# Two more scan states built by TensorE from diagonals that transfers spread, and all turns of h made by transfers

## The chip, the cores and the metric

The kernel runs on one core of one Trainium2 chip. The metric is the device time of one execution in microseconds (us), median of several runs; lower is better. TensorE (PE), VectorE (DVE), ScalarE (ACT), GpSimd (POOL) and the queue of transfers on SyncE (SP) work side by side and meet only at semaphores.

## The reference, cut to what matters

```python
# x (4, 512, 512), ctx (4, 512, 256); d_inner 512, 16 states, dt_rank 16; F = 2048
u   = silu(conv1d(ctx @ in_proj^T) + conv_b)                 # (b, 512 channels, 512 steps)
dt_low, Bm, Cm = split(x_proj @ u)                           # 16 + 16 + 16 rows by 512 steps
dt  = softplus(dt_proj @ dt_low + dt_bias);  A = -exp(A_log)
for l in steps:                                              # for each of 512 channels, 16 states
    state = state * exp(dt[l] * A) + dt[l] * u[l] * Bm[l]
    y[l]  = sum_over_states(state * Cm[l])
x1  = x + tanh(g_xattn) * swap((y + D * u) * silu(layernorm(x)))
out = x1 + tanh(g_ffn) * ffn(layernorm(x1))
# ffn: rmsnorm, 8-bit rounding of rows, ternary weights;
#      h = silu(gate) * up (2048 wide), rounded by its row's maximum, then down (2048 -> 512)
```

## The kernel before

**Units.** The scan is cut into 16 units `s` (`UNITS`), one for each batch `b = s // 4` and group of 128 channels. A unit has 16 states `n`, each a tile of 128 channels by 512 steps. For each state ACT takes the exponential exp(dt A) (L1169, into a PSUM bank), something makes dt u B, DVE runs the recurrence (`tensor_tensor_scan`, L1510), the result is multiplied by C, and PE sums it over the states into `pY` by transposing it there (L515). In text below "scan 7" is the scan of state 7.

**Who makes dt u B.** POOL does it for two states at a time (`times_b`, L889), from a copy of B spread over the partitions (`b_bc`). From unit 5 on (`PE_FROM`) states 4 and 5 (`PE_PAIR = 2`) are made by PE (`db_state`, L562): `duT`, the turned product of dt and u, times a diagonal matrix with B on it (`diag_b`), whose four blocks for each state ACT writes once a batch (`diagonal`, L1200). For these states the exponential goes to SBUF (L1163) and the product to the PSUM bank.

**Who multiplies by C.** DVE for the states 2, 3, 6, 7, 10, 14, 15 (`own`; L1518, with C spread by PE, `c_bcast`, L509), POOL for the pairs 0, 2, 4, 6 (L881) and for state 11 alone (L895).

**The feed-forward part** runs one tile of 128 rows behind: in unit `s` tile `t1 = s - 4` gets its gate and up products (L584), its silu (L1117) and the product with up (`times_up`, L1461); tile `t2 = s - 5` gets its row maximum (`h_max`, L1465), is scaled and rounded on ACT (`scale_h`, L1150), turned by PE in four groups of four blocks (`hq_transpose`, L615), and copied as bf16 to `hqT` by ACT (`copy_hqT`, L1155); tile `s - 6` gets its down product (L633) in the pieces called `fill`, and its output (L1486). For the last tiles (`DMA_FROM = 11` on) the turning is done by a transfer (`turn_h`, L410).

**Order.** All orders are written out by hand: each engine has one list, of which the loops below print the core. In units 5, 6, 7, 9, 10, 11, 13, 14, 15 the tile x is turned early (L578); units 4, 8, 12 start a batch of the feed-forward part (`t1 % NT == 0`), and their lists differ. ACT's exponential for state n waits for the scan three before it (its bank). SP's queue issues the row loads of the next unit, the four broadcasts of B and of C at the end of a batch (`load_b`, `load_c`), and the stores.

Of the kernel before, what the change touches and what calls it, by code (L numbers as in the profile page):

```python
# [5 lines left out]
F32 = mybir.dt.float32  # L6
# [6 lines left out]
P = 128  # L13
# [42 lines left out]
PE_PAIR = 2  # L56
ALONE = 11


def alone(s, n):  # L60
    return s >= PE_FROM and n == ALONE

# [21 lines left out]
def pool_pairs(s):  # L84
    return [c for c in range(NCH) if s < PE_FROM or c != PE_PAIR]

# [9 lines left out]
def by_pe(s, n):  # L96
    return s >= PE_FROM and n // CH == PE_PAIR

# [9 lines left out]
def osc(t):  # L108
# [6 lines left out]
    k_abs k_abv k_ws k_wm k_p1 k_p3 k_clip  # L115
    d_xz0 d_xz1 d_xr0 d_xr1 d_bbc0 d_bbc1 d_bbc2 d_bbc3 d_c0 d_c1 d_c2 d_c3 d_u0 d_u1 d_out0 d_out1
    s_exp s_dbu s_scan s_mul s_pmul s_pytr s_cb s_ytr s_du s_skip s_skd s_dup s_duT s_diag s_dbp s_amul s_aytr d_ca s_sz s_szp s_szT s_y s_x1
    f_bn f_sum f_dev f_ve f_rr f_xn f_xs f_e f_xm f_xqp f_xqT f_gate f_silu f_up f_h f_sq f_mh f_rh f_hs f_hm
    f_hqp f_hqT f_hb f_hp f_hqD f_dn f_o e_y e_x1 e_sq e_max e_ss""".split()
# [13 lines left out]
def build(nc, x, ctxT, g_x, g_f, w_in, w_conv, b_conv, w_xp, w_dt, b_dt, a_log, d_skip, w_gate, w_up, w_down,  # L133
          bc_rows, u_rows, out):
    with ExitStack() as stack:
# [19 lines left out]
        diag_d = sb("diag_d", [P, P])  # L155
# [42 lines left out]
        h_alone = carve(area_f, 4096, L)  # L198
        c_alone = carve(area_f, 7680, L)
# [8 lines left out]
        diag_b = [b_bc[:, CH * PE_PAIR + i, :].rearrange("p (k l) -> p k l", k=NT) for i in range(CH)]  # L208
# [14 lines left out]

        hb = [u_all[:, 2 + 2 * i:4 + 2 * i, :].rearrange("p n l -> p (n l)").bitcast(BF16) for i in range(2)]
# [63 lines left out]
        def _(sp):  # L288
# [14 lines left out]
            def load_c(b):  # L303
                for j, pair in enumerate(pooled(NT * b)):
                    if b and j < len(pooled(NT * b - 1)):
                        sp.wait_ge(S["s_pmul"], POOLED_AT[NT * b - 1] + j + 1)
# [3 lines left out]
            def load_c_alone(b):  # L310
                if b == 1:
# [16 lines left out]
            def load_b(b, quarters=range(4)):  # L328
                for q in quarters:
                    if b:  # L330
                        sp.wait_ge(S["s_dbu"], db_count(b * NT - 1, 2 * q + 1))
                    first = 4 * q + (CH if b * NT >= PE_FROM and 2 * q == PE_PAIR else 0)
                    sp.dma_start(b_bc[:, first:4 * q + 4, :], bc_rows[b, first:4 * q + 4, :].partition_broadcast(P)).then_inc(S[f"d_bbc{q}"], 16)
# [1320 lines left out]
```

## Time and profile before

| | |
|---|---|
| median of 3 runs | 612.5 us (611.86 to 614.23) |
| the profiled execution | 611.89 us, span of its instructions 609.9 us |
| busy share of the span | PE 85%, PE weight loads 59%, DVE 91%, ACT 83%, POOL 85% |
| DMA | 66.32 MB, mean 109 GB/s |
| granted TensorE clock, mean | 0.966 |

Busy time counts instructions, not waits. One unit of the steady part takes 30.3 us, one that starts a batch 33.2 us. "Idle before" in a row is the time that an engine waited just before it, and the name behind it the instruction that ended the wait. Rows of a timeline start with the start time and the busy time; where an engine's instructions overlap, the next can start a little before the one before has ended.

### The profile page before, as it was taken

What the parts mean: (1) busy time and instruction counts of PE and PEld (TensorE: products, weight loads), DVE (VectorE), ACT (ScalarE), POOL (GpSimd) and SP (SyncE); (2) the same over time, 40 slices, a digit from 0 to 9 for tenths busy, and PEclk for the clock granted to TensorE, in tenths of its full rate; (3) what the DMA queues carried; (4) which work ended last, traced back from release to release, by engine and by line L of the source; (5) the groups of instructions that cost most, each with busy time, mean ns of one, the idle gap of its engine ahead of it and who ended that gap; (6) DMA issues with size and microseconds to landing.
All of it is one profiled execution on the core that took longest, in us unless ns stands there. A gap on an engine that the chain in (4) does not pass through costs nothing. (4 is left out here: it accounts for less than half of the span.)

```text
span 609.9 us, 9603 instructions
## 1 busy us (share of the span) xinstructions
PE 516.7 (85%) x3190; PEld 359.8 (59%) x3190; DVE 556.6 (91%) x766; ACT 507.7 (83%) x776; POOL 521.0 (85%) x298
## 2 busy tenths in 40 slices
PE   6999676768675888989879898989789999998997
PEld 2443265747564676767656767675667575764443
DVE  1899989999999899999899999998999999988774
ACT  3879788986999789899978898998798989777773
POOL 1558799999999899999999899999998999973340
PEclk9999859778799999999999999999999999999999
DMA  8992951530661010115521111145411110000323
GB/s 273 403 412 108 325 197 34 192 136 1 240 243 53 0 53 2 35 34 208 203 93 35 34 37 36 35 157 223 121 35 35 36 36 18 1 18 21 84 53 86
DMA packets 38866, 66.32 MB, mean 109 GB/s; under 512 B 12177, under 2 KB 20369, under 8 KB 36002
## 3 DMA queue, kind: packets, MB, share of 16 engines
q1 hardware_dynamic: 38818, 65.72, 30.9%
q8 instruction: 25, 0.41, 0.3%
q14 instruction: 23, 0.19, 0.1%
HBM read 55.49 MB, written 8.13 MB: 104 GB/s over the span
## 5 line engine op out<-in xcount | busy, mean ns | idle before, releaser
L889 POOL TENSOR_TENSOR area_s<-area_s,b_bc 128x1024 f32<-128x1024 f32 x117 | 275.2, 2364 | 14.1 <-DVE u_all L1510 9.9
L515 PE MATMUL pY<-ident,area_s 128*128 128x128 f32 x532 | 87.9, 291 | 54.5 <-DVE area_s L1518 54.5
L584 PE MATMUL pG<-wq_gu,area_f 128*128 128x512 fp8e4 x448 | 108.0, 380 | 4.2 <-ACT area_f L1106 2.9
L1510 DVE TENSOR_TENSOR_SCAN area_s<-pA,area_s 128x512 f32<-128x512 f32 x88 | 105.1, 1205 | 5.1 <-ACT pA L1169 5.1
L515 PEld LDWEIGHTS pY<-ident,area_s 128*128 128x128 f32 x532 | 62.2, 146 | 75.4 <-DVE area_s L1518 67.9
L1169 ACT ACTIVATE pA<-dt_all,a_neg 128x512 f32<-128x512 f32 x145 | 97.7, 682 | 10.7 <-DVE area_s L1510 5.9
L881 POOL TENSOR_TENSOR u_all<-u_all 128x1024 f32<-128x1024 f32 x44 | 103.9, 2361 | 0.2 <-DMA u_all<-bc_rows 0.2
L1518 DVE TENSOR_TENSOR area_s<-area_s,pC 128x512 f32<-128x512 f32 x132 | 87.0, 661 | 0.9 <-DVE area_s L1510 0.8
L509 PE MATMUL pC<-ident,xdT 128*128 128x128 f32 x528 | 84.2, 288 | 3.2 <-DVE area_s L1518 2.0
L584 PEld LDWEIGHTS pG<-wq_gu,area_f 128*128 128x128 bf16 x448 | 41.6, 98 | 48.9 <-ACT area_f L1106 5.2
L509 PEld LDWEIGHTS pC<-ident,xdT 128*128 128x128 f32 x528 | 65.4, 146 | 8.1 <-DVE area_s L1518 6.6
L633 PE MATMUL pT<-wq_dn,area_f 128*128 128x512 fp8e4 x224 | 53.9, 379 | 0.0
L515 PE MATMUL pY<-ident,u_all 128*128 128x128 f32 x352 | 49.6, 287 | 1.7 <-POOL u_all L881 1.7
L515 PEld LDWEIGHTS pY<-ident,u_all 128*128 128x128 f32 x352 | 42.9, 149 | 5.0 <-POOL u_all L881 2.1
L1461 DVE TENSOR_TENSOR area_f<-area_f,pG 128x512 f32<-128x512 f32 x52 | 34.6, 677 | 8.4 <-PE pG L584 6.0
L1169 ACT ACTIVATE pC<-dt_all,a_neg 128x512 f32<-128x512 f32 x57 | 38.9, 683 | 3.3 <-DVE u_all L1510 2.4
L1510 DVE TENSOR_TENSOR_SCAN u_all<-pA,area_s 128x512 f32<-128x512 f32 x33 | 39.5, 1210 | 0.1
L1117 ACT ACTIVATE area_f<-pG,sm 128x512 f32<-128x512 f32 x52 | 34.3, 684 | 4.2 <-PE pG L584 3.3
L834 POOL TENSOR_TENSOR area_s<-area_s 128x511 f32<-128x511 f32 x16 | 20.0, 1273 | 20.8 <-DVE area_s L1348 20.8
L615 PE MATMUL pG<-ident,area_f 128*128 128x128 f32 x176 | 24.0, 278 | 15.9 <-ACT area_f L1155 13.1
L1510 DVE TENSOR_TENSOR_SCAN area_s<-pC,area_s 128x512 f32<-128x512 f32 x29 | 35.0, 1205 | 1.4 <-ACT pC L1169 1.4
L633 PEld LDWEIGHTS pT<-wq_dn,area_f 128*128 128x128 bf16 x224 | 21.9, 98 | 19.7
(218 smaller groups left out, 1123.0 us busy)
## 6 DMA issues: line engine op xcount, KB each, us to landing
b_bc<-bc_rows SPq DMA_DIRECT2D x14, 1024.0 KB, 6.7
area_s<-x SPq DMA_DIRECT2D x32, 256.0 KB, 2.9
u_all<-bc_rows SPq DMA_DIRECT2D x14, 512.0 KB, 6.5
b_bc<-w_gate SPq DMA_DIRECT2D x1, 4096.0 KB, 14.0
dt_all<-x SPq DMA_DIRECT2D x1, 4096.0 KB, 24.3
area_f<-w_up SPq DMA_DIRECT2D x1, 4096.0 KB, 33.6
area_f<-w_down SPq DMA_DIRECT2D x1, 4096.0 KB, 14.9
out<-area_f SPq DMA_DIRECT2D x16, 256.0 KB, 2.1
```

What stands on the lines that cost most here:

```text
L509: mm = pe.transpose(c_bank(s, m)[:, k * P:(k + 1) * P], xdT[:, s // NT, k, NS + n:NS + n + 1].to_broadcast([P, P]), ident[:, :])
L515: mm = pe.matmul(pY[:, k * P:(k + 1) * P], src[:, k * P:(k + 1) * P], ident[:, :], is_transpose=True, start=(first and k == 0), stop=(last ...
L584: mm = pe.matmul(bank, xqT[t % 2][:, k, :], wq_gu[:, k, m, c * GW:(c + 1) * GW], start=(k == 0), stop=(k == NT - 1))
L615: mm = pe.transpose(banks[r % 2][:, k * P:(k + 1) * P], h_of(t)[:, (4 * r + k) * P:(4 * r + k + 1) * P], ident[:, :])
L633: mm = pe.matmul(pT[:, :], hqT[t % 2][:, k, :], wq_dn[:, k, :], start=(k == 0), stop=(k == FK - 1))
L881: gp.tensor_tensor(hp[j], hp[j], c_bc[j], ALU.mult).then_inc(S["s_pmul"], 1)
L889: gp.tensor_tensor(db[c % NDB], du[s % 2].rearrange("p (a l) -> p a l", a=1).to_broadcast([P, CH, L]), b_bc[:, CH * c:CH * c + CH, :], ALU ...
L1117: act.activation(h_of(t)[:, c * GW:(c + 1) * GW], bank, ACT.Silu, scale=col(CS[t % 2])).then_inc(S["f_silu"], 1)
L1169: act.activation(exp_bank(s, n), dt_all[:, s, :], ACT.Exp, scale=a_neg[:, s % NT, n:n + 1]).then_inc(S["s_exp"], 1)
L1461: dve.tensor_tensor(chunk, chunk, bank, ALU.mult).then_inc(S["f_h"], 1)
L1510: dve.tensor_tensor_scan(h, at, dbu, 0.0, ALU.mult, ALU.add).then_inc(S["s_scan"], 1)
L1518: dve.tensor_tensor(p_st[i % NH], h_st[i % NH], c_bank(s, m), ALU.mult).then_inc(S["s_mul"], 1)
```

## The change

States 6 and 7 join 4 and 5: from unit 5 on PE makes dt u B of four states, and POOL of six pairs. The diagonal matrices are no longer written by ACT: in DRAM a tensor `b_spread` is filled with zeros once, then four transfers a batch write the 512 numbers of each state's B onto the diagonals, one number at a time (`spread_b`), and one transfer of 1 MB loads the sixteen blocks (`load_diagonals`). Every h tile up to 10 is turned by two transfers (`turn_whole`), from bf16 halves that ACT writes in place over the f32 ones (`whole_h`); the four groups of PE transposes and the four ACT copies are gone. The diagonal of D is written once for each of the four channel groups and no longer for each unit (`skip`). The products with C are shared out as before. Some PE steps change place: state 7's sum goes behind the gate products, and the broadcasts at a batch's end are issued in another order, behind the two turns.

```diff
-PE_PAIR = 2
-ALONE = 11
+PE_PAIRS = (2, 3)
+BY_PE = tuple(CH * c + i for c in PE_PAIRS for i in range(CH))
+NB = len(BY_PE)
+ALONE = (11,)
...
-        diag_d = sb("diag_d", [P, P])
+        diag_d = sb("diag_d", [P, NT, P])
+        zeros = sb("zeros", [P, L])
...
-        diag_b = [b_bc[:, CH * PE_PAIR + i, :].rearrange("p (k l) -> p k l", k=NT) for i in range(CH)]
+        diag_b = [b_bc[:, n, :].rearrange("p (k l) -> p k l", k=NT) for n in BY_PE]
...
+        h_int = [carve(area_f, 1024 * i, F // 4, BF16) for i in range(2)]
...
+            def zero_spread():
+                sp.wait_ge(S["k_zero"], 1)
+                sp.dma_start(b_spread.rearrange("b j (p f) -> p (b j) f", p=P),
+                             zeros[:, :].rearrange("p (a f) -> p a f", a=1).to_broadcast([P, (BATCH - 1) * NB, L])).then_inc(S["c_zero"], 16)
+
+            def spread_b(b):
+
+                sp.wait_ge(S["c_zero"], 16)
+                for j, n in enumerate(BY_PE):
+                    spots = b_spread[b - 1, j].rearrange("(k r) -> k r", k=NT)[:, 0:P * P:P + 1]
+                    sp.dma_start(spots, bc_rows[b, n].rearrange("(k p) -> k p", k=NT), allow_slow_non_contiguous=True).then_inc(S[f"c_bd{b}"], 16)
+
+            def load_diagonals(b):
+                sp.wait_ge(S[f"c_bd{b}"], 16 * NB)
                 if b == 1:
-
-                    sp.wait_ge(S["k_p3"], 2 * NW + 1)
+                    sp.wait_ge(S["s_dbu"], db_count(PE_FROM - 1, PE_PAIRS[-1]))
                 else:
-                    sp.wait_ge(S["s_amul"], b * NT - PE_FROM)
-                sp.dma_start(c_alone, bc_rows[b, NS + ALONE].partition_broadcast(P)).then_inc(S["d_ca"], 16)
+                    sp.wait_ge(S["s_dbp"], NB * (b * NT - PE_FROM))
+                sp.dma_start(b_bc[:, BY_PE[0]:BY_PE[0] + NB, :].rearrange("p j (k l) -> p (j k) l", k=NT),
+                             b_spread[b - 1].rearrange("j (k p l) -> p (j k) l", k=NT, p=P)).then_inc(S["d_bd"], 16)
...
+            zero_spread()
             load_x(3)
             load_u(3)
+            spread_b(1)
+            def turn_whole(t):
+
+                past(sp, S["f_dn"], t - 1)
+                for i in range(2):
+                    past(sp, S["f_hqD"], 32 * t + 16 * i)
+                    sp.wait_ge(S["f_ha"], 2 * t + i + 1)
+                    sp.dma_start_transpose(hqT[t % 2][:, i * FK // 2:(i + 1) * FK // 2, :], h_int[i]).then_inc(S["f_hqD"], 16)
+
             for s in range(NT, UNITS):
                 load_z(s)
                 load_x(s)
                 load_u(s)
+                b = s // NT
                 if s % NT == 0:
-                    load_b(s // NT)
-                    load_c(s // NT)
-                    load_c_alone(s // NT)
+                    load_b(b, (0, 1))
+                if s >= 6:
+                    turn_whole(s - 6)
+                if s % NT == 0:
+                    if b > 1:
+                        load_diagonals(b)
+                    load_b(b, (2,))
+                    load_c(b, (0,))
+                    load_b(b, (3,))
+                    load_c(b, (1, 2, 3))
+                    load_c_alone(b)
+                if s == NT:
+                    load_diagonals(1)
+                if s in (NT + 1, NT + 2):
+                    spread_b(s - NT + 1)
                 if s >= 7:
                     store(s - 7)
...
-                pe.wait_ge(S["s_diag"], CH * NT * (s // NT - 1) + NT * (i + 1))
+                pe.wait_ge(S["d_bd"], 16 * (s // NT))
...
                 if t1 % NT:
                     pe.wait_ge(S["f_h"], FC * t1)
                     xq_transpose(t1, pG[0])
+                if s >= PE_FROM:
+                    db_state(s, 2)
                 fill(s, early, 4)
                 y_sum(s, 3)
                 c_bcast(s, 6)
+                if s >= PE_FROM:
+                    db_state(s, 3)
                 y_sum_pooled(s, 0)
-                if t2 >= 0:
-                    if t1 % NT:
-                        pe.wait_ge(S["f_xqT"], t1 + 1)
-                    hq_transpose(t2, 0, pG)
-                    hq_transpose(t2, 1, pG)
                 fill(s, 4, DPARTS)
-                if t2 >= 0:
-                    hq_transpose(t2, 2, pG)
-                    hq_transpose(t2, 3, pG)
                 y_sum(s, 6)
...
                 if t1 % NT:
                     y_sum_pooled(s, 1)
                     c_bcast(s, 10)
-                    y_sum(s, 7)
                     gate(t1, 2)
                     gate(t1, 3)
                 else:
 
                     c_bcast(s, 10)
-                    y_sum(s, 7)
-                    if ALONE in own(s):
-                        c_bcast(s, ALONE)
+                    if s < PE_FROM:
+                        y_sum(s, 7)
+                        c_bcast(s, 11)
                     gate(t1, 2)
                     gate(t1, 3)
                     y_sum_pooled(s, 1)
+                if s >= PE_FROM:
+                    y_sum(s, 7)
                 y_sum(s, 10)
...
-                if s + 1 < UNITS:
+                if 3 in pool_pairs(s + 1) and s + 1 < UNITS:
                     times_b(s + 1, 3)
...
-                if t <= UNITS - NT:
-                    past(act, S["f_hqp"], HR * (t - (1 if t < UNITS - NT else 2)) + HR)
-                else:
+                if t < UNITS - NT and t and c % 2 == 0:
+                    act.wait_ge(S["f_hqD"], 32 * (t - 1) + (32 if c else 16))
+                elif t > UNITS - NT:
                     act.wait_ge(S["f_hb"], 2 * (t - 2 - DMA_FROM) + 2)
...
-            def copy_hqT(t, r, banks):
-                act.wait_ge(S["f_hqp"], HR * t + r + 1)
-                past(act, S["f_dn"], t - 1)
-                act.activation(hqT[t % 2][:, 4 * r:4 * r + 4, :], banks[r % 2].rearrange("p (k t) -> p k t", t=P),
-                               ACT.Copy, bias=-MAGIC).then_inc(S["f_hqT"], 1)
+            def whole_h(t, i):
+
+                act.wait_ge(S["f_hm"], 2 * t + i + 1)
+                act.activation(h_int[i], h_main[:, i * F // 2:(i + 1) * F // 2], ACT.Copy, bias=-MAGIC).then_inc(S["f_ha"], 1)
...
-                    if n == 1:
-                        skip(s)
...
+                    if n in (6, 7) and t2 >= 0:
+                        whole_h(t2, n - 6)
                     if n in (5, 6) and t2 >= 0:
                         scale_h(t2, n - 5)
...
-                    if n in (7, 8) and t2 >= 0:
-                        copy_hqT(t2, 2 * n - 14, pG)
-                        copy_hqT(t2, 2 * n - 13, pG)
...
                 if by_pe(s, n):
-                    dve.wait_ge(S["s_dbp"], CH * (s - PE_FROM) + n % CH + 1)
+                    dve.wait_ge(S["s_dbp"], NB * (s - PE_FROM) + BY_PE.index(n) + 1)
```

## Rows read from the trace of the kernel before

**Rows 1.** The page, part 1: busy time of each engine over the span
```profile
PE 516.7 (85%) x3190; PEld 359.8 (59%) x3190; DVE 556.6 (91%) x766; ACT 507.7 (83%) x776; POOL 521.0 (85%) x298
```
**Rows 2.** Units 10, 11, 12: length, busy PE, PEld, DVE, ACT, POOL; clock, DMA
```profile
369.00:399.20 30.20, 27.45 (x193) 20.23 (x192) 29.71 (x40) 27.18 (x45) 30.12 (x17) 1.00 0.12 36
399.20:429.80 30.60, 27.41 (x194) 20.29 (x192) 28.63 (x35) 27.61 (x47) 30.25 (x16) 1.00 0.59 205
429.80:463.00 33.20, 27.63 (x194) 20.38 (x193) 32.27 (x49) 27.59 (x47) 30.92 (x18) 1.00 0.18 57
```
**Rows 3.** Waits of DVE from 182.6 to 551 us: total, times, longest
```profile
DVE area_f L1461 <- PE pG L584: 6.0, 8, 1.5
DVE area_s L1510 <- ACT pA L1169: 3.2, 6, 1.1
DVE area_s L1510 <- ACT pC L1169: 1.4, 3, 0.8
```
**Rows 4.** Groups of instructions: busy, mean ns | idle before, releasers
```profile
L889 POOL TENSOR_TENSOR area_s<-area_s,b_bc 128x1024 f32<-128x1024 f32 x117 | 275.2, 2364 | 14.1 <-DVE u_all L1510 9.9 <-DMA b_bc<-bc_rows 3.0
...
L1150 ACT ACTIVATE area_f<-area_f,sm 128x1024 f32<-128x1024 f32 x24 | 27.4, 1142 | 4.1 <-DVE sm L1479 4.1
...
L1155 ACT ACTIVATE area_f<-pG 128x512 bf16<-128x512 f32 x44 | 23.4, 584 | 0.0
L1123 ACT ACTIVATE area_f<-area_f 128x2048 bf16<-128x2048 f32 x12 | 22.9, 1911 | 7.9 <-DVE area_f L1461 7.9
```
**Rows 5.** Timeline of PE in unit 10: start us, busy us, instructions, idle before
```profile
366.73 0.66 PE L515 MATMUL pY<-ident,area_s 128*128 128x128 f32 x4 [1.37 <-DVE area_s L1518]
...
370.07 1.06 PE L562 MATMUL pC<-b_bc,area_s 128*128 128x128 f32 x8
...
376.10 1.04 PE L515 MATMUL pY<-ident,u_all 128*128 128x128 f32 x8
376.97 1.06 PE L615 MATMUL pG<-ident,area_f 128*128 128x128 f32 x8
```
**Rows 6.** Timeline of DVE in unit 10: scans 6 and 7, 10, 14
```profile
376.85 2.31 DVE L1510 TENSOR_TENSOR_SCAN area_s<-pA,area_s 128x512 f32<-128x512 f32 x2
...
381.90 1.20 DVE L1510 TENSOR_TENSOR_SCAN area_s<-pA,area_s 128x512 f32<-128x512 f32 x1
...
390.59 1.22 DVE L1510 TENSOR_TENSOR_SCAN area_s<-pC,area_s 128x512 f32<-128x512 f32 x1 [0.31 <-ACT pC L1169]
```
**Rows 7.** Timeline of ACT in unit 10: exponential 8, scaling, exponentials 12 and 13, silu 2
```profile
376.97 0.69 ACT L1169 ACTIVATE pC<-dt_all,a_neg 128x512 f32<-128x512 f32 x1
377.59 1.13 ACT L1150 ACTIVATE area_f<-area_f,sm 128x1024 f32<-128x1024 f32 x1
...
382.38 1.45 ACT L1169 ACTIVATE pA<-dt_all,a_neg 128x512 f32<-128x512 f32 x2
...
387.00 0.69 ACT L1117 ACTIVATE area_f<-pG,sm 128x512 f32<-128x512 f32 x1
```
**Rows 8.** Timelines of PE and DVE in unit 12: state 10's sum, up products, first times_up
```profile
452.13 0.60 PE L515 MATMUL pY<-ident,area_s 128*128 128x128 f32 x4
452.57 1.89 PE L584 MATMUL pG<-wq_gu,area_f 128*128 128x512 fp8e4 x8
...
453.63 0.69 DVE L1461 TENSOR_TENSOR area_f<-area_f,pG 128x512 f32<-128x512 f32 x1 [0.52 <-PE pG L584]
```
**Rows 9.** Line 410, the turns by transfer: issue ns min/median/max, and landing
```profile
L410 SPq DMA_TRANSPOSE area_f<-u_all x8: 1232/1236/1347, 562.7 to 597.3; - x8
...
DMA to landing us min/median/max: 3.0/3.1/3.1
```
**Rows 10.** The page, part 3: SP's transfers, packets, MB, share of 16 engines
```profile
q1 hardware_dynamic: 38818, 65.72, 30.9%
```
**Rows 11.** Timelines: load of u for unit 3, and POOL's product that reads it
```profile
130.24 0.45 SPq L301 DMA_DIRECT2D u_all<-u_rows  x1
...
144.04 1.27 POOL L876 TENSOR_TENSOR area_s<-dt_all,u_all 128x512 f32<-128x512 f32 x1
```

More of the change, by code:

```diff
@@ L55, with alone_count @@
 PE_FROM = PLAIN + 1
-PE_PAIR = 2
-ALONE = 11
+PE_PAIRS = (2, 3)
+BY_PE = tuple(CH * c + i for c in PE_PAIRS for i in range(CH))
+NB = len(BY_PE)
+ALONE = (11,)
 def alone(s, n):
-    return s >= PE_FROM and n == ALONE
+    return s >= PE_FROM and n in ALONE
+def alone_count(s, n):
+    return len(ALONE) * (s - PE_FROM) + ALONE.index(n)
 def own(s):
@@ L84, in pool_pairs @@
 def pool_pairs(s):
-    return [c for c in range(NCH) if s < PE_FROM or c != PE_PAIR]
+    return [c for c in range(NCH) if s < PE_FROM or c not in PE_PAIRS]
 DB_AT = [sum(len(pool_pairs(i)) for i in range(s)) for s in range(UNITS + 1)]
@@ L96, in by_pe @@
 def by_pe(s, n):
-    return s >= PE_FROM and n // CH == PE_PAIR
+    return s >= PE_FROM and n in BY_PE
 VE, RR, M2, REC1, XS, SS, RH, M3, REC2, FAC, MH, XSUM, DEV = range(13)
@@ L133, in build @@
 def build(nc, x, ctxT, g_x, g_f, w_in, w_conv, b_conv, w_xp, w_dt, b_dt, a_log, d_skip, w_gate, w_up, w_down,
-          bc_rows, u_rows, out):
+          bc_rows, u_rows, b_spread, out):
     with ExitStack() as stack:
@@ L301, in load_u, with load_c @@
                 sp.dma_start(u_in[s % 2], u_rows[s]).then_inc(S[f"d_u{s % 2}"], 16)
-            def load_c(b):
+            def load_c(b, pairs=range(NP)):
                 for j, pair in enumerate(pooled(NT * b)):
+                    if j not in pairs:
+                        continue
                     if b and j < len(pooled(NT * b - 1)):
@@ L329, in load_b @@
                 for q in quarters:
+                    if q == 1 and b * NT >= PE_FROM:
+                        continue
                     if b:
                         sp.wait_ge(S["s_dbu"], db_count(b * NT - 1, 2 * q + 1))
-                    first = 4 * q + (CH if b * NT >= PE_FROM and 2 * q == PE_PAIR else 0)
-                    sp.dma_start(b_bc[:, first:4 * q + 4, :], bc_rows[b, first:4 * q + 4, :].partition_broadcast(P)).then_inc(S[f"d_bbc{q}"], 16)
+                    sp.dma_start(b_bc[:, 4 * q:4 * q + 4, :], bc_rows[b, 4 * q:4 * q + 4, :].partition_broadcast(P)).then_inc(S[f"d_bbc{q}"], 16)
             def store(t):
@@ L630, in down @@
                 for k in range(part * DK, min(part * DK + DK, FK)):
-                    if k == FK // 2 and t >= DMA_FROM:
-                        pe.wait_ge(S["f_hqD"], 32 * (t - DMA_FROM) + 32)
+                    if k == FK // 2:
+                        pe.wait_ge(S["f_hqD"], 32 * t + 32)
                     mm = pe.matmul(pT[:, :], hqT[t % 2][:, k, :], wq_dn[:, k, :], start=(k == 0), stop=(k == FK - 1))
@@ L741, in _ @@
                 z_transpose(s)
-                if ALONE in own(s):
-                    y_sum(s, ALONE)
+                if s < PE_FROM:
+                    y_sum(s, 11)
                 y_sum_pooled(s, 2)
@@ L827, in _ @@
             gp.memset(neg_half[:, :], -0.5).then_inc(S["k_const"], 1)
+            gp.memset(zeros[:, :], 0.0).then_inc(S["k_zero"], 1)
             gp.wait_ge(S["k_const"], 9)
@@ L1257, in _ @@
                             x_variance(t1 + 1)
-                    if n in (3, 4) and s % NT == NT - 1 and s + 1 < UNITS:
-                        for k in range(NT):
-                            diagonal(s // NT + 1, n - 3, k)
                     if n == 5 and t1 % NT == 0:
@@ L1649 @@
     u_rows = nc.dram_tensor("u_rows", (UNITS, P, L), F32, kind="Internal").ap()
+    b_spread = nc.dram_tensor("b_spread", (BATCH - 1, NB, NT * P * P), F32, kind="Internal").ap()
     out = nc.dram_tensor("out", _OUT, F32, kind="ExternalOutput").ap()
-    build(nc, *aps, bc_rows, u_rows, out)
+    build(nc, *aps, bc_rows, u_rows, b_spread, out)
     r = run_bass_kernel_spmd(nc, [arrays], core_ids=[0])
```

102 lines of the change are left out of this document (45 added, 57 removed).

## The prediction, made before the changed kernel ran

> **What bounds the kernel now.** I read the page first: DVE has the largest busy share, 91%, with ACT, POOL and PE at 83 to 85% [rows 1]. Such shares average over the start and the tail, so the busy time by stretch comes next. In unit 10 DVE is busy 29.71 of 30.20 us and POOL 30.12; in unit 11 DVE 28.63 of 30.60 and POOL 30.25; in unit 12, which has more DVE work, DVE 32.27 of 33.20 and POOL 30.92 [rows 2]. Two engines look full, and who leads is told by the waits. From 182.6 to 551 us DVE waits for named instructions 6.0 + 3.2 + 1.4 = 10.6 us in all, never for POOL [rows 3]. POOL's products with B did wait, 14.1 us over the run, 9.9 of them for DVE's scans [rows 4]. So DVE sets the pace and POOL trails it with its buffers full; POOL at 30.1 to 30.3 us a unit just fits. DVE's waits are for an exponential (the scan of state 14, 0.31 us in unit 10 [rows 6]) and for an up product. Both end one loop: exponential 13 waits for scan 10 to free its bank (381.90 + 1.20; the pair of exponentials that ends with it takes 382.38 to 383.83), then follow a table load, four silus, a table load and exponential 14. The clock is 1.00 in these units and PE about 91% busy [rows 2].
>
> **The change part by part.**
>
> *POOL loses one product a unit* (units 5 to 15): 2.36 us each [rows 4], 26 us in all. No DVE wait ends on POOL, so this is worth 0. Its bounds are 0 and the whole of DVE's named waits, and the row nearest is 0.
>
> *DVE* has the same instructions. Scans 6 and 7 now read the exponential from SBUF and the product from PSUM, as scans 4 and 5 do: 0.
>
> *PE* loses sixteen transposes, two stretches like the 1.06 us one at 376.97, and gains two `db_state`, each like the 1.06 us one at 370.07 [rows 5]: work and so clock stay. What moves is when. Before unit 10's state-0 pair is summed (376.10) PE has run from 366.73, where it was released by DVE's last product of unit 9, without a pause that a row shows, 9.37 us [rows 5]. `db_state(2)` goes into that stretch, `db_state(3)` to its end. Eight such instructions take 0.87 to the next start (376.10 to 376.97), db's own I take as 0.89. So `db_state(3)` starts at 376.99 and, 1.06 later, is ready at 378.05, seen by DVE at about 378.09. Scan 7 started at 376.85 + 1.11 = 377.96 (two overlapping scans, 2.31 for both [rows 6]). Scan 7 is late by 0.13 us. Units 6, 7, 9, 10, 11, 13, 14, 15 have this order: 8 x 0.13 = 1.0 us. Unit 5 has shorter fillers, units 8 and 12 more DVE work ahead of scan 7: 0 there. Bounds: 0 (a pitch 0.1 smaller) and 0.3 a unit (2.4 us).
>
> *ACT* loses four copies of 0.584 and gains two passes over 1024 columns in bf16. No row shows this form. From below half of the 2048-column bf16 pass, 0.96; from above the f32 pass of 1024 columns, 1.14 [rows 4]. The nearest is the latter less what bf16 seems to save, 1.06; starts follow 0.04 to 0.09 earlier than ends (a busy 0.69 at 376.97 leads to a start at 377.59 [rows 7]), so I count 1.04 each, and the same for `scale_h`. New order behind exponential 8 (376.97): `whole_h(0)` at 377.59, `scale_h(1)` 378.63, exponential 9 at 379.67 to 380.35 (scan 9 starts one scan before 381.90, fine), `whole_h(1)` 380.29, exponential 10 at 381.33 to 382.02. Scan 10 started at 381.90 and is 0.13 late anyway: 382.03. Just hidden; with passes at 1.14 it is 0.2 us a unit in the nine units 5 to 7, 9 to 11, 13 to 15, 1.8 us. The diagonals of D and B that ACT no longer writes stand where no DVE wait ends: 0.
>
> *The loop from scan 10* keeps its length. Gate product 2 waits for silu 0, not for state 7's sum, so putting that sum behind the gates brings nothing; in nine units the sum fits before state 10's, which waits for DVE. In units 8 and 12 it stands behind the pooled sum and in front of the up product, for which DVE already waits 0.52: 452.13 to 452.57, 0.44 us each [rows 8]. There ACT's chain also carries two passes (2.08) for four copies (1.90 from start to start): 0.18. 2 x 0.62 = 1.2 us; bounds 0 and 2.
>
> *The turns.* SP issues the first when `whole_h(0)` is done, 378.7; it lands 3.1 later, 381.8; the second waits for that and for `whole_h(1)` (381.4) and lands at 385.0 [rows 9]. Silu 2, which overwrites the second half, started at 387.00 [rows 7]: 2.0 us to spare. The down product needs them only in the next unit. Ahead of the turns in SP's queue stand loads that are released at the unit's start, and at a batch's end 1 MB of B. Behind them wait the diagonals and the rest of B and C; the first use of the diagonals is db_state(0) of the next unit, at about 370.07 - 0.9 + 30.3 = 399.5 on unit 10's clock, 14 us after 385.0 [rows 5]; B and C are used by POOL, whose reserve grows. 0.
>
> *The other transfers.* By the mean packet, 0.309 x 16 x 609.9 / 38818 = 78 ns of one engine [rows 10], the zero fill (1536 packets of 2 KB) is 7.5 us on sixteen engines, behind w_down and ahead of the load of u for unit 3, which has 13.8 us [rows 11]: hidden. Spreading one batch is 2048 packets of 4 bytes, 10 us on sixteen engines; the diagonals are 2048 packets of 512 B, 10 us, once a batch. Hidden. POOL's extra memset falls before its first wait: 0. The tail keeps its turns and sums: 0.
>
> **Sum.** 1.0 + 0 + 1.2 = +2.2 us. On the profiled execution (span 609.9 and 2.0 around it, 611.9) this is 614.1; on the median of the runs, 0.6 above it, 614.7. I take the middle, 614.4. All terms at their ends, the two stalls of the nine units added, are 0 and 2.4 + 1.8 + 2 = 6.2 us: 611.9 to 618.7.
>
> **Rivals.**
> *A, faster.* The engines beside DVE have more room: POOL 2.4 us a unit, PE no longer stops for ACT's copies, and ACT writes no diagonals. If that shortens DVE's waits by half, 10.6 / 2 = 5.3: 607. All of them gone is 602, and no more is to be had. For: POOL is 99% busy in unit 10. Against: the loop starts at scan 10, which none of this brings forward.
> *B, slower: the turns come late.* One mechanism: silu 2 waits for the second turn. It decides once a turn takes over 3.1 + 1.0 = 4.1 us from issue to landing, since two follow one another; each 0.1 beyond costs 0.2 us in each of 11 units. At 4.5 us: 0.8 x 11 = 8.8, 623. For: in units 7 and 11 it runs beside 1 MB loads, and the 3.1 is from the tail, where the queue is empty. Against: in the other units the row loads are long landed.
> *C, slower: the spreading holds the queue.* If a spread transfer, whose slowest dimension has length 4, runs on four engines and its packets cost the mean 78 ns, one batch takes 512 x 0.078 = 40 us there. Batch 3's is issued behind the turns of unit 5. On unit 10's clock that is 385.0, so it ends at 425.0; the next unit's second turn lands 3.1 later, 428.1, and its silu 2 is wanted at 387.00 + 30.3 = 417.3 [rows 7]. It would wait 10.8 us: 625. It decides once the spreading takes over 417.3 - 3.1 - 385.0 = 29.2 us, 57 ns a packet. Against: packets of 4 bytes should be far cheaper than the mean, which is one of 1.7 KB.
> *D, small stalls at their upper ends*: more than 615.6, about 617.
> *E, all hidden*: the pitch of PE is a tenth shorter and nothing happens, 612.
>
> The Trainium skill ("DMA: Bandwidth & Descriptors", section "Why a DMA increments its semaphore by 16 and not by 1") says that a transfer runs on as many engines, up to 16, as divide the slowest dimension of both sides; by that rule it is four here, which is C's first condition. No row here shows the share of engines of such a transfer; if the rule holds and the packets are cheap, the sum stays.
>
> **How the numbers follow.** What a measurement of this kernel can tell from no change is about 0.5%, 3.06 us: 609.4 to 615.6. Forecast 0.50 (of it 0.06 above 615.6), E 0.10, A 0.10 (0.08 of it below 609.4), D 0.15, B 0.10, C 0.05. Faster 0.08; same 0.44 + 0.10 + 0.02 = 0.56; slower 0.06 + 0.15 + 0.10 + 0.05 = 0.36. The range 610.5 to 619.5 takes in both bounds of the sum, and leaves out most of A and nearly all of B and C, about 0.2. The likeliest case's own range is 612 to 616.5.
>
> **What would show it.** In unit 10 of the changed kernel: POOL 2.4 us less busy and idle before products with B; DVE busy unchanged within 0.1; a wait of DVE at scan 7 for PE's L562-like products of 0.1 to 0.2 us; none or up to 0.2 at scan 10; still 0.3 at scan 14 for the exponential; the passes `whole_h` at 1.06; turns at 3.1 us to landing and no wait of silu 2 for a transfer; in units 8 and 12 DVE's wait for the up product near 1.1 instead of 0.52. I am wrong if a DVE wait shrinks by over 3 us in total, if ACT's silu waits for a transfer, or if a spread transfer takes tens of us to land.

## The result: slower by 1.35%, because TensorE fell to half clock six times

The changed kernel takes 622.15 us (median of 4 runs, 617.06 to 623.09) against 612.64 for the kernel before on the same chip: ratio 1.0135 by the means (1.0155 by the medians), 95% interval 1.0076 to 1.0194. The forecast was 614.4, and the range of 610.5 to 619.5 does not hold the time. The changed kernel's runs spread more than those of before, and they go with the granted clock: 617.06 at a mean of 0.964, 621.59 at 0.950, 622.71 and 623.09 at 0.945. The profiled run is the one at 623.09 (span 621.3, clock 0.945; before 609.9, clock 0.966); the six stretches at half clock are those of this run.

Part 1 of the page after:
```profile
PE 522.5 (84%) x3190; PEld 368.0 (59%) x3190; DVE 557.8 (90%) x766; ACT 496.7 (80%) x718; POOL 496.5 (80%) x288
```
Against [rows 1] POOL lost 24.5 us, ACT 11.0, DVE gained 1.2, and PE shows 5.8 us more for the same 3190 instructions: the same work took longer.

The same units as [rows 2] (length, busy PE, PEld, DVE, ACT, POOL, then granted clock, DMA share and GB/s) and five more, units 5 to 13 without unit 6:
```profile
215.00:246.70 31.70, 27.89 (x201) 22.43 (x200) 29.28 (x39) 26.88 (x42) 28.04 (x16) 0.95 0.22 43
...
277.20:309.20 32.00, 28.62 (x194) 21.11 (x192) 28.66 (x35) 24.80 (x36) 27.45 (x15) 0.95 0.71 243
309.20:345.00 35.80, 30.91 (x194) 22.75 (x193) 32.34 (x48) 27.41 (x43) 28.55 (x17) 0.86 0.20 55
345.00:376.90 31.90, 28.76 (x194) 21.46 (x193) 30.14 (x41) 27.09 (x42) 28.14 (x16) 0.95 0.20 51
376.90:407.30 30.40, 27.00 (x194) 20.54 (x192) 29.90 (x40) 26.87 (x42) 28.02 (x16) 1.00 0.22 53
407.30:437.75 30.45, 27.01 (x194) 20.65 (x193) 28.74 (x36) 24.77 (x36) 27.56 (x15) 1.00 0.75 237
437.75:471.70 33.95, 28.25 (x194) 21.56 (x193) 32.28 (x49) 27.36 (x43) 28.60 (x17) 0.95 0.27 75
471.70:503.70 32.00, 28.67 (x194) 21.18 (x192) 30.02 (x41) 27.00 (x42) 28.03 (x16) 0.95 0.19 50
```
Read the clock column first. Units 10 and 11 have 1.00 and take 30.4, where they took 30.3 and 30.6. Every unit that grew by more than 0.4 us has a clock under 1.00. Units 5 to 14 together, ten units of the kernel before and the same ten after:
```profile
214.31:523.66 309.35, 274.90 (x1929) 203.88 (x1928) 300.35 (x397) 274.30 (x448) 302.81 (x161) 1.00 0.21 72
```
```profile
215.00:534.12 319.12, 281.23 (x1929) 212.81 (x1928) 301.30 (x397) 266.03 (x401) 280.59 (x151) 0.96 0.31 90
```
319.12 - 309.35 = 9.8 of the span's 11.4 us arise here, with the same number of instructions on PE and DVE.

The length of each unit, from one `gated_y` (the product of DVE that stands once a unit and ends it) to the next, worked out from the starts in the timelines. A star marks a unit in which the trace's record of the granted clock has a stretch at half the full clock, the 1.2 GHz level; each such stretch lasts 3.4 us except where a number stands. The lower rows are experiments told below; "best kernel" is the fastest of them:

```
unit              5       6      7      8            9       10     11      12      13      14     sum
before            30.34   30.35  30.33  33.17        30.34   30.34  30.62   33.17   30.35   30.34  309.35
after             31.72*  30.44  32.08* 35.80*(10.2) 31.82*  30.45  30.44   33.91*  32.02*  30.44  319.12
idle, old places  30.35   30.44  30.43  33.52        30.44   30.44  30.43   33.53   30.44   30.43  310.45
turns alone       30.36   30.36  30.35  35.75*(10.2) 31.75*  30.35  30.37   34.63*(6.8) 30.36 32.02* 316.30
idle at start     31.83*  30.44  30.44  34.00*       30.45   30.44  31.85*  34.01*  30.44   30.44  314.34
best kernel       29.75   30.00  29.80  32.49        29.75   29.99  29.75   32.50   29.75   29.97  303.75
best, no idle     29.75   29.96  29.75  34.29*(6.8)  29.76   29.97  29.76   32.88*  29.75   29.97  305.84
```

Now the place. Timeline of PE after, unit 10 (clock 1.00), start and busy us, in brackets the idle time before and its releaser:
```profile
388.83 1.89 PE L641 MATMUL pG<-wq_gu,area_f 128*128 128x512 fp8e4 x8
390.56 1.04 PE L572 MATMUL pY<-ident,u_all 128*128 128x128 f32 x8
392.96 0.65 PE L566 MATMUL pC<-ident,xdT 128*128 128x128 f32 x4 [1.36 <-DVE area_s L1542]
394.00 1.90 PE L641 MATMUL pG<-wq_gu,area_f 128*128 128x512 fp8e4 x8 [0.38 <-ACT area_f L1162]
```
and of unit 7 of the same trace:
```profile
290.86 1.04 PE L572 MATMUL pY<-ident,u_all 128*128 128x128 f32 x8
293.26 0.65 PE L566 MATMUL pC<-ident,xdT 128*128 128x128 f32 x4 [1.37 <-DVE area_s L1542]
294.29 3.53 PE L641 MATMUL pG<-wq_gu,area_f 128*128 128x512 fp8e4 x8 [0.38 <-ACT area_f L1162]
```
The same two stops, 1.36 and 0.38 us. In unit 10 the eight gate products behind them take 1.90 us, in unit 7 3.53. The windows of unit 7 around it (columns as above; the clock is the seventh value behind the length):
```profile
287.00:290.60 3.60, 3.39 (x21) 1.87 (x19) 3.60 (x5) 3.60 (x5) 3.60 (x3) 1.00 0.38 73
290.60:294.00 3.40, 1.94 (x14) 1.35 (x12) 3.40 (x4) 3.19 (x5) 3.32 (x3) 1.00 0.58 90
294.00:297.40 3.40, 3.11 (x8) 1.24 (x9) 2.69 (x4) 2.20 (x4) 3.40 (x2) 0.56 1.02 296
297.40:300.80 3.40, 3.40 (x22) 2.29 (x22) 0.84 (x2) 2.85 (x4) 3.40 (x3) 0.94 1.00 392
```
The clock is 1.00 before the stop and while PE waits, 0.56 in the 3.4 us in which PE is busy again. DVE pays, in the same unit: its first product with an up product waits 2.96 us, where the one of unit 10 (clock 1.00) does not wait. In unit 7 of the kernel before it waited 0.84. Unit 7 after, unit 10 after, unit 7 before:
```profile
299.65 0.69 DVE L1484 TENSOR_TENSOR area_f<-area_f,pG 128x512 f32<-128x512 f32 x1 [2.96 <-PE pG L641]
```
```profile
397.72 0.68 DVE L1484 TENSOR_TENSOR area_f<-area_f,pG 128x512 f32<-128x512 f32 x1
```
```profile
295.27 0.69 DVE L1461 TENSOR_TENSOR area_f<-area_f,pG 128x512 f32<-128x512 f32 x1 [0.84 <-PE pG L584]
```
At a batch's start the stop is longer, and the clock stays down 10.2 us (unit 8 after):
```profile
322.65 1.12 PE L572 MATMUL pY<-ident,area_s 128*128 128x128 f32 x4 [3.02 <-DVE area_s L1542]
...
326.16 3.59 PE L641 MATMUL pG<-wq_gu,area_f 128*128 128x512 fp8e4 x8 [0.69 <-ACT area_f L1151]
```
Where do these stops come from? PE's waits (engine, line waited for: total us, times, longest), before and after, from 183.3 to 561.7:
```profile
PE pY L515 <- DVE area_s L1518: 22.8, 23, 3.5
PE pG L615 <- ACT area_f L1155: 13.1, 11, 1.8
...
PE pC L509 <- DVE area_s L1518: 2.0, 3, 0.8
```
```profile
PE pY L572 <- DVE area_s L1542: 28.2, 25, 3.5
PE pC L566 <- DVE area_s L1542: 14.2, 12, 1.4
```
Before, PE waited 13.1 us for ACT between the halves of the transposes of h, about a third into a unit. With the transposes gone PE is through early and meets DVE's pace further on, mostly at one instruction, C's broadcast for state 10, which needs the bank that DVE's product of an earlier state frees: 2.0 us became 14.2. The idle time was mostly moved, not increased (46.0 us by all of PE's waits before, 50.2 after). And DVE's waits answer [rows 3]; in the ten units alone they sum to 7.0 us before and 15.7 after, 8.7 of the 9.8 us:
```profile
DVE area_f L1484 <- PE pG L641: 15.4, 11, 3.0
DVE area_s L1542 <- issue: 1.9, 1, 1.9
DVE area_s L1534 <- ACT pA L1213: 1.4, 4, 0.4
DVE area_s L1534 <- ACT pC L1213: 0.9, 3, 0.3
```

### The profile page after: what moved, and what is told of

Same layout as the page of the kernel before. It is cut to its first block and busy times, and to the rows that moved or that the text cites. A ratio compares the mean times of both kernels' runs of the same rounds, so it can differ in the third digit from the quotient of the medians.

```text
span 621.3 us, 9506 instructions
## 1 busy us (share of the span) xinstructions
PE 522.5 (84%) x3190; PEld 368.0 (59%) x3190; DVE 557.8 (90%) x766; ACT 496.7 (80%) x718; POOL 496.5 (80%) x288
## 5 line engine op out<-in xcount | busy, mean ns | idle before, releaser
L933 POOL TENSOR_TENSOR area_s<-area_s,b_bc 128x1024 f32<-128x1024 f32 x106 | 249.5, 2362 | 49.1 <-DVE u_all L1534 44.4
L641 PE MATMUL pG<-wq_gu,area_f 128*128 128x512 fp8e4 x448 | 115.9, 400 | 7.4 <-ACT area_f L1162 4.4
L572 PEld LDWEIGHTS pY<-ident,area_s 128*128 128x128 f32 x532 | 64.7, 150 | 83.5 <-DVE area_s L1542 72.0
L566 PE MATMUL pC<-ident,xdT 128*128 128x128 f32 x528 | 84.9, 289 | 14.9 <-DVE area_s L1542 14.2
L1213 ACT ACTIVATE pA<-dt_all,a_neg 128x512 f32<-128x512 f32 x131 | 87.5, 678 | 8.6 <-DVE area_s L1534 7.5
L1534 DVE TENSOR_TENSOR_SCAN area_s<-pA,area_s 128x512 f32<-128x512 f32 x74 | 88.6, 1207 | 3.4 <-ACT pA L1213 2.6
L641 PEld LDWEIGHTS pG<-wq_gu,area_f 128*128 128x128 bf16 x448 | 44.0, 101 | 55.4 <-issue 8.1
L1195 ACT ACTIVATE area_f<-area_f,sm 128x1024 f32<-128x1024 f32 x24 | 27.4, 1140 | 10.5 <-DVE sm L1502 10.5
L1213 ACT ACTIVATE pC<-dt_all,a_neg 128x512 f32<-128x512 f32 x49 | 33.2, 679 | 2.2 <-DVE u_all L1534 1.0
L1207 ACT ACTIVATE area_s<-dt_all,a_neg 128x512 f32<-128x512 f32 x44 | 30.7, 708 | 0.0
```

Source lines behind the costliest of these rows:

```text
L566: mm = pe.transpose(c_bank(s, m)[:, k * P:(k + 1) * P], xdT[:, s // NT, k, NS + n:NS + n + 1].to_broadcast([P, P]), ident[:, :])
L572: mm = pe.matmul(pY[:, k * P:(k + 1) * P], src[:, k * P:(k + 1) * P], ident[:, :], is_transpose=True, start=(first and k == 0), stop=(last ...
L641: mm = pe.matmul(bank, xqT[t % 2][:, k, :], wq_gu[:, k, m, c * GW:(c + 1) * GW], start=(k == 0), stop=(k == NT - 1))
L933: gp.tensor_tensor(db[c % NDB], du[s % 2].rearrange("p (a l) -> p a l", a=1).to_broadcast([P, CH, L]), b_bc[:, CH * c:CH * c + CH, :], ALU ...
L1207: act.activation(db[n // CH][:, n % CH, :], dt_all[:, s, :], ACT.Exp, scale=a_neg[:, s % NT, n:n + 1]).then_inc(S["s_exp"], 1)
L1213: act.activation(exp_bank(s, n), dt_all[:, s, :], ACT.Exp, scale=a_neg[:, s % NT, n:n + 1]).then_inc(S["s_exp"], 1)
```

## The experiments

The theory: stops of TensorE in the middle of the unit, uncovered when the transposes of h left, are followed by stretches at half clock, and these make nearly all of the loss. The rivals: the transfers (11 MB and 32,300 packets more on SP's queue) slow something; the states 6 and 7 through PE cost more than reckoned; the new order as such makes new waits.

**Idle work in the old places.** Sixteen transposes of the identity into a free bank, eight where each pair of `hq_transpose` stood; the transfers stay.
```
                 y_sum_pooled(s, 0)
+                if s >= PE_FROM: idle_work(s, 2)     # 8 transposes of ident, result unused
                 fill(s, 4, DPARTS)
+                if s >= PE_FROM: idle_work(s, 2)
                 y_sum(s, 6)
```


> The changed kernel with sixteen idle transposes of the identity (into the free bank pG1) in each unit from 5 on, at the two places where h was turned by TensorE before: eight behind the sum of pair 0, eight ahead of the sum of state 6. Theory (clock): the 9.5 us of loss are six stretches at half the granted clock, 3.4 us long and once 10 us, which begin when TensorE runs out of work between the sum of state 6 and the gate products 2 and 3; with work there the clock stays 1.00 from unit 5 on, units take 30.3 to 30.6 and 33.2 to 33.9 us, and the time is 612 to 615. Rival 1 (late operands): the up products are late because turns, gates or silus are late, and more work on TensorE makes them later still: 622 or more, with the waits of VectorE for up products still near 15 us. Rival 2 (a new wait at scan 7): unchanged, about 622.

Measured: 613.34 us (10 runs, 612.52 to 614.38), ratio 1.0014, interval 1.0000 to 1.0028; clock of the profiled run 0.972. From unit 5 the clock record has no stretch at half clock until the last microseconds. The ten units and the waits of DVE:
```profile
213.65:524.10 310.45, 285.70 (x2089) 224.69 (x2088) 300.95 (x396) 265.42 (x401) 280.73 (x151) 1.00 0.32 92
```
```profile
DVE area_f L1493 <- PE pG L641: 8.3, 9, 1.5
DVE area_s L1543 <- ACT pA L1222: 2.0, 6, 0.4
DVE area_s L1543 <- ACT pC L1222: 1.0, 3, 0.4
```
The clock is 1.00 and work that computes nothing gives back 8.7 us of 9.8. That this is the clock, and not some other effect of the idle work on PE's order, is borne out by the changed kernel itself: its four units without a stretch (6, 10, 11, 14) take 30.44 or 30.45 us, as they do here with the idle work. What is left, +1.1 us over ten units, is the change without its clock trouble. PE's wait at C's broadcast for state 10 is 2.7 us again.

**Idle work ahead of gate 0 only**, eight transposes a unit.
```
+                if s >= PE_FROM: idle_work(s, 2)
                 gate(t1, 0)
```


> The changed kernel with eight idle transposes in each unit from 5 on, all in one place, just ahead of gate product 0. They shorten the 1.36 us stop ahead of the broadcast for state 10 to about 0.5 us, not the 3.0 us stop ahead of the sum of state 6 in the units that start a batch. Theory (clock): most of the half-clock stretches of the plain units go, that of units 8 and 12 may stay: 613 to 618. Rivals: as for the sixteen, no gain, 622.

Measured: 614.90 us (613.71 to 616.46), 1.0046, interval 1.0031 to 1.0060. One stretch is left from unit 5 on, in unit 12 (34.32 us). Half the idle work, put close ahead of the place, does most of it; what remains is at a batch's start, where the stop is the long one.

**The turns by transfer, without state 3's pair on PE.** `PE_PAIRS = (2,)`; products with B for states 6 and 7 on POOL as before.


> Only states 4 and 5 by TensorE, as before the change (POOL makes seven pairs again), but h turned by transfers and the diagonals spread by transfers. TensorE has 1.8 us less work a unit than either kernel. Theory (clock): still more or longer half-clock stretches than the changed kernel, 622 to 630. Rival (the two more states are the cost, by their wait at scan 7 or by the transfers that serve them): back to 612 to 614.

Measured: 621.07 us (620.56 to 623.71), 1.0154, interval 1.0128 to 1.0181. The whole loss, with four stretches at half clock:
```profile
214.82:531.12 316.30, 263.14 (x1769) 193.18 (x1768) 300.84 (x396) 266.78 (x401) 303.45 (x161) 0.96 0.31 91
```
Its undisturbed plain units take 30.35 to 30.37, the time of before within 0.02 (but for unit 11, which took 30.62), so in these the clock is the whole of the loss. Units 8 and 12 both have a stretch and can't be split in this way, and of the 9.6 us by which the span is longer 2.1 lie behind unit 14, where no stretch stands before the very end.

**The states on PE, h turned by PE and ACT as before.** `hq_transpose` and `copy_hqT` are back in their places, `turn_whole` and `whole_h` gone.


> Four states by TensorE and diagonals by transfers, but h turned by TensorE and copied by ScalarE, as before the change. TensorE has 1.8 us more work a unit than either kernel, 29.3 of 30.3 us. Theory (clock): no half-clock stretch from unit 5 on, mean clock 0.96 or more; the time is 612 to 616, above the kernel before only by what the fuller TensorE makes late (scan 7, gates). Rival (the two more states are the cost): 618 to 622.

Measured: 614.82 us (614.10 to 615.81), 1.0043, interval 1.0028 to 1.0058; no stretch at half clock in units 5 to 14, units of 30.43 and 33.60. The clock loss belongs to the turns; this half costs the small stalls, 30.43 - 30.34 and 33.60 - 33.17, together 1.2 us over the ten units. The rest of the 2.4 us by the medians lies outside them.

**Idle work at the unit's start.** Twelve transposes ahead of the previous unit's last sum, where PE also stands still, from unit 6 on.
```
                 if s > PLAIN:
+                    if s > PE_FROM: keep_on(s) three times     # 4 transposes each
                     y_sum(s - 1, 15)
```


> The changed kernel with twelve idle transposes in each unit from 6 on, at another place: ahead of the sum of state 15 at the unit's start, where TensorE stands idle for 1.4 us in both kernels. Nearly as much added work as the sixteen of the first run, in a stop that the change did not make. Theory (the stop in the middle of the unit lets the clock fall): half-clock stretches stay, 617 to 622. Rival (it is TensorE's work over the whole unit that counts, wherever it lies): no half-clock stretch, 613 to 615.

Measured: 619.30 us (616.97 to 622.27), 1.0126, interval 1.0081 to 1.0170; five stretches at half clock between 194 and 450 us. Two of them lie in units 4 and 5, where this run has no idle work. In units 6 to 14 there are three, where the changed kernel has five, and they cost 2.4 us against the first experiment, where the changed kernel loses 7.3; the stops of 1.36 and 0.38 us are still there in its unit 10. So work in another place helps in part, and less than the eight transposes close ahead of the stop (614.90, no run above 616.46; here none below 616.97): the place counts, and it is not shown that it is all that counts.

**State 3's product with C given to POOL.** The change had freed 2.4 us a unit of POOL, and DVE sets the pace: 0.66 us a unit should come off. In this and all later kernels with this product on POOL, state 7's sum also stands ahead of gate products 2 and 3 again in the units that start a batch. First with POOL's product right behind its pair 0 and 24 idle transposes, then without idle work:
```
-ALONE = (11,)
+ALONE = (3, 11)                      # states whose product with C is POOL's, summed alone
+                if s >= PE_FROM: times_c_alone(s, 3)     # POOL, behind times_c(s, 0)
+                    y_sum_alone(s, 3); idle_work(s, 3)   # PE, behind y_sum_pooled(s, 0)
```


> A try at a version that beats both: sixteen idle transposes raised to twenty-four at the same two places, and from unit 5 on state 3's product with C goes from VectorE to GpSimd (0.58 us a unit less on VectorE, 1.27 more on GpSimd, 0.88 less work on TensorE ahead of its products for states 6 and 7); in the units that start a batch state 7's sum is back ahead of the gates. Theory (VectorE sets the pace once the clock holds, GpSimd has 2.3 us of room): 11 x 0.58 = 6.4 us less than the first run, 606 to 608. Rival (the loop from scan 10 over the silus to exponential 14 sets it, with ScalarE): 611 to 613.

> The same with no idle transposes. Theory (clock): TensorE has a longer stop in the middle of the unit than in the changed kernel, so half-clock stretches in most units from 5 on, mean clock 0.95 or less; 614 to 622, 8 to 14 us above the version with them. Rival (the clock only costs where TensorE is late, and it now has more room): within 2 us of it.

Measured: 616.32 us (615.34 to 617.24), 1.0074, interval 1.0051 to 1.0097, and 615.96 us (614.52 to 618.41), 1.0067, interval 1.0035 to 1.0099. Both are slower than before. From unit 5 on the first has no stretch at half clock and the second, without idle work, only one, in unit 12 (33.03 for 32.50). That is a miss: stretches in most units and 8 to 14 us more were expected of the second. In its unit 10 PE stops 1.07 us ahead of pair 1's sum and 1.22 ahead of pair 4's, both for POOL, and still no plain unit has a stretch. The product delays POOL's next ones, PE waits for them in its order, and DVE behind PE (first kernel, unit 10):
```profile
393.36 1.09 PE L572 MATMUL pY<-ident,u_all 128*128 128x128 f32 x8 [0.83 <-POOL u_all L935]
...
397.08 0.69 DVE L1496 TENSOR_TENSOR area_f<-area_f,pG 128x512 f32<-128x512 f32 x1 [0.61 <-PE pG L641]
```
Plain units take 30.9 (unit 11 takes 30.4), 0.5 more than without the product: the 0.66 us is paid back with 0.5 on top. Units 8 and 12 take 32.50 for 33.52.

**The product later.** POOL does state 3 just before state 11, with 16 idle transposes in the old places; the second run also moves the sum of POOL's third pair behind the up products.
```
                 if s >= PE_FROM:
+                    times_c_alone(s, 3)          # POOL, behind times_b(s + 1, 1)
                     times_c_alone(s, 11)
```


> Sixteen idle transposes at the old places, state 3's product with C on GpSimd as in the last try, but now late: just ahead of state 11's, so that GpSimd's product for pair 4 is not pushed back by 1.27 us. In the last try TensorE waited 0.83 us for that product ahead of up product 2, and VectorE then 0.6 us for it. Theory (that order was the loss, the load of GpSimd is not): plain units of about 29.9 us, 606 to 609. Rival (GpSimd is full again at 29.3 of 30.4 us and holds whatever stands last): 612 to 615.

> As the run beside it, and TensorE sums pair 4 behind up product 3, so that no up product stands behind GpSimd. Theory: as the run beside it or up to 2 us less, 605 to 609. Rival (GpSimd full): 612 to 615, now with the wait at the sum of a unit's end.

Measured: 613.01 us (612.27 to 614.54), 1.0021, interval 1.0009 to 1.0032, and 614.64 us (612.35 to 615.01), 1.0043, interval 1.0021 to 1.0064. Waits of DVE in the first:
```profile
DVE area_f L1496 <- PE pG L641: 7.8, 9, 1.5
DVE area_s L1554 <- DVE u_all L1546: 5.7, 8, 0.8
```
and the timelines of its unit 10 around one of the eight:
```profile
396.71 0.66 PE L572 MATMUL pY<-ident,area_f 128*128 128x128 f32 x4 [0.58 <-POOL area_f L951]
...
397.64 0.60 PE L566 MATMUL pC<-ident,xdT 128*128 128x128 f32 x4
...
398.33 0.69 DVE L1554 TENSOR_TENSOR area_s<-area_s,pC 128x512 f32<-128x512 f32 x1 [0.80 <-DVE u_all L1546]
```
The second line names DVE's own scan as releaser, but that ended 0.8 us earlier. What came last is PE's broadcast of C for state 15 (397.64 + 0.60), in PE's queue behind the sum for which POOL was late. In the second run the same wait is 6.3 us, in 10.

**The two single sums behind that broadcast.**
```
                     up(t1, 3)
-                    y_sum_alone(s, 3); y_sum_alone(s, 11)
                     y_sum(s, 14)
                     c_bcast(s, 15)
+                    y_sum_alone(s, 3); y_sum_alone(s, 11)
```


> State 3's product on POOL late in the unit, with 16 idle transposes in the old places of the removed ones, as in the run that gave 613.0 (1.0021). There PE reached C's broadcast for state 15 only behind the two sums for which POOL multiplies (a stop of 0.58 us), and DVE's product of state 15 waited 0.80 us for it in 8 units, 5.7 us in all. Here these two sums stand behind state 14's sum and the broadcast for state 15. Theory (that order is the cost, and DVE gains the product it gave away): the wait goes and 0.6 to 0.8 us a unit comes off in 8 to 9 units, 5 to 7 us: 606 to 608. Rival (POOL, with one more product of 1.2 us a unit, is full, and the wait only moves to a product with B or to the next unit's pooled sum): 611 to 613, with a DVE wait of over 5 us by another name.

Measured: 607.64 us (6 runs, 606.83 to 609.09), ratio 0.9925, interval 0.9902 to 0.9948. This beats both kernels. The 5.7 us are gone from the list, DVE does 550.5 us of work for 557.8, and from unit 5 on nothing is at half clock until the last microseconds:
```profile
215.54:519.29 303.75, 283.11 (x2048) 220.05 (x2047) 294.66 (x386) 265.30 (x401) 292.65 (x161) 1.00 0.33 96
```
Its control has idle work as in the first experiment and state 11's sum behind the broadcast for state 15; no product is moved to POOL, and state 7's sum stays behind the gates.


> The changed kernel with 16 idle transposes in the old places (613.3, 1.0014) and only state 11's sum moved behind the broadcast for state 15; POOL has no product more. Theory (without the second sum PE does not stop there long enough for DVE to wait): as before within 0.3%, 612 to 614. Rival (the stop of PE at state 11's sum already cost DVE time in the changed kernel): 609 to 611.

Measured: 613.33 us (612.18 to 615.18), 1.0023, interval 1.0009 to 1.0037, units of 30.44: this order alone is worth nothing. The gain of the best kernel over it is 5.7 us by the medians; over the ten units it is 310.45 - 303.75 = 6.7 us against the first experiment. That ten products of 0.66 us on DVE make 6.6 is in part chance: plain units gain 0.44 to 0.69, and units 8 and 12 gain 1.03 each. There the sum of state 7 stands ahead of the gates again, and DVE's wait for the first up product in unit 12 falls from 0.88 to 0.45 us. No run has that step alone. The difference from the medians lies ahead of unit 5, whose start varies between the traces (212.6 to 215.6).

**The best kernel without idle work.**


> The kernel that gave 607.6 (0.9925: state 3's product on POOL late in the unit, both single sums behind the broadcast for state 15, 16 idle transposes a unit), without the idle transposes. Theory (TensorE's stops, not filled, are followed by stretches at half the granted clock): one to five such stretches from unit 5 on, granted clock 0.945 to 0.965 instead of 0.969, 2 to 8 us more: 610 to 616. Rival (the idle work is worth nothing once PE has no stop at the single sums): within 1 us of 607.6 and no stretch at half clock.

Measured: 610.56 us (12 runs, 609.27 to 615.04), 0.9976, interval 0.9958 to 0.9995. The ten units:
```profile
213.91:519.75 305.84, 271.10 (x1888) 204.13 (x1887) 294.88 (x387) 265.50 (x401) 292.31 (x161) 0.98 0.33 95
```
Plain units are as in the best kernel to 0.05 us; unit 8 is 1.80 longer and unit 12 0.38, the two with a stretch at half clock. Idle work is worth 2.9 us here, by the medians. The mid-unit stops at C's broadcast are back (13.8 us in 12 waits, where the changed kernel has 14.2 in 12), and yet no plain unit of the profiled run has a stretch.

## Why the prediction was wrong

**The step that failed** is in the paragraph on PE: "work and so clock stay. What moves is when". The work stayed (1929 instructions in the ten units, both times), the when moved, and the clock did not stay. I derived the clock from the amount of work, while the clock fell behind stops in the middle of a unit. Filling these stops held it. The prediction itself said that PE "no longer stops for ACT's copies" (rival A) and took it for relief; the question where PE would stop instead was not asked. It could be worked out: [rows 5] show PE running 9.37 us without pause into the transposes, and [rows 7] when silu and exponentials come; with two stretches of transposes and the wait between them replaced by two `db_state` that stand earlier, PE starts its first gate products 11.97 us into unit 10 (388.83 - 376.86) where it was 13.19 (382.03 - 368.84), and so stands at C's broadcast for state 10, which DVE releases. The price by the ten units: 319.12 - 310.45 = 8.7 us, six stretches, 0.4 to 1.65 us for one of 3.4 us and 2.3 for the one of 10.2. The paragraph gives no row for the step from work to clock; the sum has no term for the clock, and the range no room for one.

**Scans 6 and 7 behind `db_state(3)`: +0.13 a unit.** Right in mechanism and nearly in size. Timeline of DVE after, unit 10:
```profile
384.88 2.39 DVE L1534 TENSOR_TENSOR_SCAN area_s<-area_s,pA 128x512 f32<-128x512 f32 x2
```
2.31 became 2.39 [rows 6]; units at full clock grew by 0.10. With the turns alone they did not grow at all, with the states alone by 0.09, so the term is db's.

**Scan 10's exponential just hidden: 0.** Right, no wait in unit 10; scan 14 waits 0.33 (0.31 in [rows 6]). `whole_h` took 1.04, reckoned as 1.06.

**Units 8 and 12: +0.62 each.** They are 0.35 longer with the clock held (33.52 and 33.53 against 33.17). Right place, size too large: DVE's wait for the first up product of unit 12 grew by 0.36 (0.52 to 0.88 with the clock held), where 0.62 was reckoned.

**Unit 11** became 0.18 shorter, 30.44 for 30.62, which I had not foreseen. Together the quiet part of the sum, forecast at 2.2 (0.13 of it in unit 15), measures 1.1 over units 5 to 14 (310.45 - 309.35).

**POOL's lost product: 0.** Right, and it shows again what idle room is worth: POOL waited 42.8 us for DVE from 183.3 us on, where it had waited 8.1. It paid only when DVE gave it a product.

**The transfers.** Right in effect: turns land after 3.1 us (median; 4.3 the longest), no silu waits for one, and no wait of an engine ends on the zero fill or the spreading. Not free, though: the zero fill, reckoned as 7.5 us, lands 22.6 us after its issue, and the broadcasts of B land after 9.0 us for 6.7 (medians). That the spreading might hold the queue (C) is refuted by the first experiment, which keeps every transfer and runs at the time of before, and by the trace of the changed kernel: the 2048 packets of 4 bytes of a batch start within 5.0, 7.6 and 5.4 us, at 10 ns each in the mean, where the forecast had reckoned 10 us on sixteen engines and C needed 29.2. The Trainium skill's rule ("DMA: Bandwidth & Descriptors", section "Why a DMA increments its semaphore by 16 and not by 1") on the share of engines could not be tested: the traces list no landing for these transfers and name no engine for a packet.

**The rivals.** B's 623 is the number nearest to the measurement, but its mechanism did not occur: the time agrees by chance. The case that took place was not among the rivals.

The Trainium skill ("TensorE: Matmul & The Clock Gate", section "What's actually happening") puts it as "the default state is throttled, and activity releases the throttle". The traces agree: sixteen transposes without a use restore 8.7 us. The same page (section "Why this matters for your kernels") warns of long single idle gaps. That advice does not cover what the trace shows: four of six stretches follow a stop of 1.36 us and one of 0.38 with work between them.

**What stays open** is which stops bring the clock down. Units 10 and 11 have the very stops of units 7, 9 and 13 and no stretch; the best kernel without idle work still stops at C's broadcasts (13.8 us in 12), and has no stretch in a plain unit; the kernel before stops at its batch starts too, and has none. Timeline of PE before, unit 12:
```profile
439.49 1.10 PE L615 MATMUL pG<-ident,area_f 128*128 128x128 f32 x8 [1.40 <-ACT area_f L1150]
...
443.22 1.11 PE L615 MATMUL pG<-ident,area_f 128*128 128x128 f32 x8 [1.77 <-ACT area_f L1155]
```
And the runs of the changed kernel differ by 6 us among themselves. Its run at 617.06 has a mean clock of 0.964, hardly under before's 0.966, while the kernel of the first experiment takes 613.15 at 0.960: the mean over the whole span, with start and tail, does not give the time, and no trace of the run at 617.06 was kept. The single stretches weren't steered one by one; that idle work in the place removes them is shown, their exact condition is not.

## What to carry to other kernels

When work leaves TensorE, ask where its idle time will stand, not only how much there is: behind a stop in mid-unit the work can run at half clock for some us, even while another engine sets the pace and PE stays about 88% busy. Try filling the old place with useless work first: where the time comes back with the clock at 1.00 and nothing else changed, the clock was the cause; compare with the units of the unfilled kernel that had no stretch. Room won on an engine that trails is worth nothing until the pacing engine hands it work, and then the handed work has to stand in every in-order queue behind what the pacing engine needs next.

## What was not expected of the hardware

The stretches at half clock lasted 3.4, 6.8 or 10.2 us; of the six of the changed kernel one began while PE stood still, one 0.25 us after a stop of 3.02 us, and four 0.1 to 0.9 us after the stop of 0.38. Half clock doubles matmul time nearly fully (1.90 to 3.53 us for eight of 512 columns) but costs DVE-paced work only 0.4 to 1.65 us of 3.4. And the same kernel, with the same instructions, spread from 617.06 (mean clock 0.964) to 623.09 us (0.945), where the filled one spread from 612.52 to 614.38.
